# Output projection after attention: split products in the last head, late rows last, and a later rounding of x

## What is computed

```
xn  = layernorm(x)                                  # 2048 x 1024
qkv = xn @ attn_qkvw + attn_qkvb
ctx = softmax(q k^T / sqrt(32)) v   for 32 heads     # columns side by side: 2048 x 1024
z   = xn @ A_w^T                                     # 2048 x 512
gate = softmax of the 16 largest of 64 router scores, 0 elsewhere
out = x + ctx @ attn_ow + attn_ob + 2 * (z * gate) @ B_w^T
```

## Time and profile before

| what | us |
|---|---|
| three runs, median | 2524.45 |
| the profiled execution, its own time | 2530.7 |
| its span, first to last instruction | 2528.9 |
| PE busy | 2489.5 (98%) |
| DVE / ACT / POOL busy | 1493.7 / 1224.9 / 1636.1 |
| end of the last-head matmuls | 2247.8 |
| first matmul of the output stage | 2254.6 |
| mean granted TensorE clock | 0.994 |

### The profile page before, as it was taken

The page is one execution under the profiler, slowest core; times in us unless marked ns, Lnnn a source line. Parts: engine busy times, 40 slices in busy tenths (PEclk is TensorE's granted clock), DMA queues, the critical chain, the costliest instruction groups (busy, mean ns, idle before and its releaser), DMA issues. The chain is left out here.

```text
span 2528.9 us, 34185 instructions
## 1 busy us (share of the span) xinstructions
PE 2489.5 (98%) x12856; PEld 1622.4 (64%) x12856; DVE 1493.7 (59%) x2524; ACT 1224.9 (48%) x2311; POOL 1636.1 (65%) x556
## 2 busy tenths in 40 slices
PE   7999999999999999999999999999999999989999
PEld 4788888888755555555555555555555555448887
DVE  7511110104588788788888788878888888522221
ACT  5211111110066676667666666667666766761000
POOL 0110111221079999999999999999999999962121
PEclk9999999999999999999999999999999999999999
DMA  4233335324367777777877877877777777564332
GB/s 167 92 125 124 124 115 162 102 79 125 96 158 164 150 160 165 158 151 165 165 150 158 165 153 155 167 150 161 164 159 150 166 165 151 116 158 141 116 104 88
DMA packets 174991, 359.26 MB, mean 142 GB/s; under 512 B 90432, under 2 KB 115520, under 8 KB 143808
## 3 DMA queue, kind: packets, MB, share of 16 engines
q0 software_dynamic: 22752, 165.69, 33.2%
q1 hardware_dynamic: 152096, 191.70, 26.5%
HBM read 127.42 MB, written 63.70 MB: 76 GB/s over the span
## 5 line engine op out<-in xcount | busy, mean ns | idle before, releaser
L1173 DVE TENSOR_REDUCE part_max<-ps_b 128x1 f32<-128x512 f32 x1984 | 1214.4, 681 | 263.7 <-PE ps_b L1046 263.6
L997 POOL TENSOR_TENSOR psum_p<-psum_p,probs 128x2048 f32<-128x2048 f32 x253 | 1181.8, 4671 | 53.6 <-ACT probs L1159 43.3
L1159 ACT ACTIVATE probs<-ps_b 128x512 f32<-128x512 f32 x1920 | 971.2, 621 | 351.2 <-PE ps_b L1036 345.9
L1036 PE MATMUL ps_b<-q,k 97*128 97x512 f32 x1344 | 547.6, 412 | 0.0
L1046 PE MATMUL ps_b<-k,q 96*128 96x512 f32 x1344 | 536.8, 401 | 0.6
L1036 PEld LDWEIGHTS ps_b<-q,k 97*128 97x128 f32 x1344 | 252.4, 188 | 223.4 <-issue 135.8
L1064 PE MATMUL ps_b<-probs,v 128*32 128x512 f32 x2640 | 319.4, 598 | 0.5 <-ACT probs L1159 0.5
L351 POOL TENSOR_TENSOR wlo<-wraw,whi 128x1024 fp32r<-128x1024 f32 x20 | 48.0, 2399 | 405.7 <-ACT whi L512 405.7
L1036 PE MATMUL ps_b<-qk 97*128 97x512 f32 x704 | 289.8, 414 | 2.0 <-PEq L84 1.7
L1046 PEld LDWEIGHTS ps_b<-k,q 96*128 96x128 f32 x1344 | 256.4, 191 | 49.5 <-DVE part_max L1173 17.9
L1046 PE MATMUL ps_b<-qk 96*128 96x512 f32 x640 | 254.8, 398 | 0.0
(11 more groups left out here) (128 smaller groups left out, 2572.6 us busy)
## 6 DMA issues: line engine op xcount, KB each, us to landing
psum_q<-probs POOLq DMA_DIRECT2D x158, 1024.0 KB, 7.7
qk<-qk_scr SPq DMA_DIRECT2D x66, 256.0 KB, 7.3
qk_scr<-ehi SPq DMA_DIRECT2D x16, 1024.0 KB, 3.9
qk_scr<-elo SPq DMA_DIRECT2D x16, 1024.0 KB, 6.7
k<-qk_scr SPq DMA_DIRECT2D x63, 256.0 KB, 4.1
q<-qk_scr SPq DMA_DIRECT2D x63, 256.0 KB, 8.0
wraw<-wcat SPq DMA_DIRECT2D x21, 512.5 KB, 7.4
craw<-cz_scr SPq DMA_DIRECT2D x14, 768.0 KB, 4.8
```

Of the source, the lines that this page charges most:

```text
L997: pool.tensor_tensor(acc[:, :], first[:, :], tile(h, t)[:, :], ALU.add).then_inc(pool_done, 1)
L1036: pe.matmul(ps[:, st_bank(n), :], kp[s][0:PACK + 1, t * P:(t + 1) * P], qp[s][0:PACK + 1, b * NQ:(b + 1) * NQ], start=True, stop=True).the ...
L1159: act.activation(tile(h, t)[:, b * NQ:(b + 1) * NQ], ps[:, st_bank(n), :], ACT.Exp, scale=SCALE).then_inc(exp_done, 1)
L1173: dve.tensor_reduce(part_max[hn % 2][:, tn, b:b + 1], ps[:, ring_bank(u), :], AX_X, ALU.max) \
```

## The change

- **x rounded later.** In pass n ACT does `normalise(n-1)`, then `round_x(n-3)`, then `deviation(n)`; DVE does `rest_x(n-4)` where it did `rest_x(n-3)`, and the copies of the router's query come one pass later.
- **First splits in the last head.** In head 31 ACT makes `chi` of row blocks 0 to 5 of token tile 0 after tile 6 (after `take_sums(30)`), and `whi` of weight blocks 0 and 1 after tiles 7 and 8. DVE makes the `clo` and the two `wlo` at tile 9, before the reciprocal of head 30.
- **The sums' way of head 31** moves into the output stage: ACT copies the sums there, SP spreads them behind two weight loads, the reciprocal comes after `wlo` of block 6, and the product with the raw context goes from POOL to DVE, behind `clo` of token tile 1. POOL's `normalise(30)` comes after its additions; its result is stored by SP in the output stage.
- **Late rows last.** PE does row blocks 0 to 10 of both token tiles, then row block 11 of both.
- Tiles are placed elsewhere so that the new writes touch only free memory; seven weight blocks are loaded early instead of six; PSUM is one tensor for both stages, and token tile 1 uses banks away from the sums.

```
             for n in range(TT):
-                if n >= CHUNK:
-                    round_x(n - 2)
                 if n >= 1:
                     normalise(n - 1)
+                if n >= ROUND_LAG:          # ROUND_LAG = 3
+                    round_x(n - ROUND_LAG)
                 deviation(n)
-                if 2 <= n < CHUNK:
-                    round_x(n - 2)
...
                 if n >= 1:
                     shift(n - 1)
-                if n >= 3:
-                    rest_x(n - 3)
+                if n > ROUND_LAG:
+                    rest_x(n - ROUND_LAG - 1)
                 variance(n)
-                if n >= CHUNK and n % CHUNK == CHUNK - 1:
-                    router_query(n // CHUNK - 1)
+                if n > CHUNK and n % CHUNK == 0:
+                    router_query(n // CHUNK - 2)
...
# attend, SP
-            store_ctx(LAST - 1)
-            for s in range(2):
-                sp.wait_ge(ctx_stored[s], 16 * QB * (HEADS // 2 - (LAST % 2 == s)))
-            sp.wait_ge(sums_taken, HEADS)
-            for b in range(QB):
-                sp.dma_start(sums_q[b * HD:(b + 1) * HD, :], sums_b[b * HD:b * HD + 1, :]).then_inc(last_spread, 16)
# attend, POOL
                 for t in LAST_POOL_ORDER if h == LAST else POOL_ORDER:
-                    if h == LAST and t == LAST_POOL_TILES[-1]:
-                        normalise(LAST - 1)
...
+            normalise(LAST - 1)
# attend, ACT (SPLIT_AT = SUMS_AT = 6, SPLIT_W = 2, FIRST_KT = 6, before 4)
                     if t == SUMS_AT and h >= 1:
                         take_sums(h - 1)
+                    if h == LAST and t == SPLIT_AT:
+                        act.wait_ge(ready_loaded[0], 16)
+                        act.wait_ge(pv_done, TT * (LAST - 1))
+                        act.activation(chi[:, 0, 0:FIRST_KT, :], craw[:, 0, 0:FIRST_KT, :], ACT.Copy).then_inc(chi_part, 1)
+                    if h == LAST and t - SPLIT_AT - 1 in range(SPLIT_W):
+                        k = t - SPLIT_AT - 1
+                        act.wait_ge(early_loaded, 16)
+                        act.wait_ge(sum_ready, LAST)
+                        act.activation(whi[:, k, :], w_early[:, k, :], ACT.Copy).then_inc(whi_done, 1)
             take_raw(LAST)
-            take_sums(LAST)
# attend, DVE
+                    if h == LAST and t == RECIPROCAL_AT:
+                        dve.wait_ge(chi_part, 1)
+                        dve.tensor_tensor(clo[:, 0, 0:FIRST_KT, :], craw[:, 0, 0:FIRST_KT, :],
+                                          chi[:, 0, 0:FIRST_KT, :].bitcast(F32), ALU.subtract).then_inc(clo_part, 1)
+                        for k in range(SPLIT_W):
+                            dve.wait_ge(whi_done, k + 1)
+                            dve.tensor_tensor(wlo[:, k, :], w_early[:, k, :], whi[:, k, :].bitcast(F32), ALU.subtract) \
+                                .then_inc(wlo_done, 1)
                     if t == RECIPROCAL_AT and h >= 1:
                         reciprocal(h - 1)
# output stage, SP (EARLY = 7, before 6)
-            for k in range(EARLY, EARLY + 3):
+            for k in range(EARLY, EARLY + 2):
                 load_w(k)
+            sp.wait_ge(last_taken, 1)
+            for b in range(QB):
+                sp.dma_start(sums_q[b * HD:(b + 1) * HD, :], sums_b[b * HD:b * HD + 1, :]).then_inc(last_spread, 16)
+            for k in range(EARLY + 2, OUT_KT):
+                load_w(k)
+            sp.wait_ge(ctx_ready, LAST)
+            for b in range(QB):
+                sp.dma_start(cz_scr[BOTTLENECK + (LAST - 1) * HD:BOTTLENECK + LAST * HD, b * NQ:(b + 1) * NQ],
+                             out_last[b * HD:(b + 1) * HD, :]).then_inc(ctx_stored[(LAST - 1) % 2], 16)
             sp.wait_ge(last_recip, 1)
...
# output stage, POOL
-            pool.wait_ge(last_recip_loaded, 16 * QB)
-            pool.tensor_tensor(sums_b[:, :], raw_last[:, :], recip_b[:, :], ALU.mult).then_inc(last_ready, 1)
-            pool.wait_ge(last_ready, 1)
# output stage, PE
+            def first_tiles(ks):
+                for u in range(2):
+                    for k in ks:
+...
+                        last = products(u, k)          # six matmuls, after the waits for its splits
+                    if k == OUT_KT - 1:
+                        last.then_inc(mm_ready, 1)
-            tile(0, 0, True)
-            tile(0, 1, True)
+            first_tiles(range(READY_KT))               # READY_KT = 11
+            first_tiles(range(READY_KT, OUT_KT))
# output stage, ACT
-            split_piece(0, 0)
-            split_w(0)
-            split_w(1)
-            split_piece(0, 1)
-            for k in range(2, OUT_KT):
+            act.wait_ge(sum_ready, HEADS)
+            act.wait_ge(sums_spread, 16 * QB * LAST)
+            act.activation(sums_b[:, :], ps[:, sum_bank, :], ACT.Copy).then_inc(last_taken, 1)
+            for k in range(SPLIT_W, OUT_KT):
                 split_w(k)
+                if k == FIRST_KT - 2:
+                    split_piece(0, 1)
             split_piece(1, 0)
# output stage, DVE
-            split_piece(0, 0)
-            split_w(0)
-            dve.wait_ge(last_spread, 16 * QB)
-            dve.reciprocal(recip_q[:, :], sums_q[:, :]).then_inc(last_recip, 1)
-            split_w(1)
-            split_piece(0, 1)
-            for k in range(2, OUT_KT):
+            for k in range(SPLIT_W, OUT_KT):
                 split_w(k)
+                if k == FIRST_KT - 2:
+                    split_piece(0, 1)
+                if k == FIRST_KT:
+                    dve.wait_ge(last_spread, 16 * QB)
+                    dve.reciprocal(recip_q[:, :], sums_q[:, :]).then_inc(last_recip, 1)
             split_piece(1, 0)
+            dve.wait_ge(last_recip_loaded, 16 * QB)
+            dve.tensor_tensor(sums_b[:, :], raw_last[:, :], recip_b[:, :], ALU.mult).then_inc(last_ready, 1)
```

More of the change, by code:

```diff
@@ L540, in _ @@
                     round_w(1, 1, 1)
-            round_x(TT - 2)
             normalise(TT - 1)
-            round_x(TT - 1)
+            for n in range(TT - ROUND_LAG, TT):
+                round_x(n)
             def q_part(u, blk, nb):
@@ L725, in attend @@
 def attend(nc, qk_scr, v_scr, recip_scr, cz_scr, w2, w_early, early_loaded, qk0, q12, k12, v01, part_max0,
-           z3_stored, craw, ready_loaded, tail):
+           z3_stored, craw, ready_loaded, tail, w2_split, chi, clo, split_done, seam):
     with ExitStack() as ctx:
@@ L737, in attend @@
         qp = [qk0[:, 0, :], q12[:, 0, :], q12[:, 1, :]]
[L738 to L742, removed]
+        whi, wlo = w2_split
+        psum_p, psum_q, probs = [], [], []
+        for n_tiles in (OUT_KT // 2 - 1, RING - OUT_KT // 2 + 1):
+            (psum_p if not psum_p else psum_q).append(sb(f"psum_{len(probs)}", [P, T]))
+            for _ in range(n_tiles):
+                probs.append(sb(f"probs{len(probs)}", [P, T]))
+        psum_p.append(sb("psum_p1", [P, T]))
+        psum_q.append(sb("psum_q1", [P, T]))
+        raw_last, sums_b, recip_b, sums_q, recip_q, out_last = tail
         raw_ctx = [raw_last if s == LAST % 3 else sb(f"raw_ctx{s}", [P, NQ]) for s in range(3)]
         out_ctx = [sb(f"out_ctx{s}", [P, NQ]) for s in range(2)]
+        vh = [v01[:, 0, :, :], v01[:, 1, :, :], sb("vh2", [P, TT, HD])]
         ones = sb("ones", [P, HD])
@@ L1203, in _, with project_output @@
                         take_transposed(h + 1)
-def project_output(nc, x, w2, bias, cz_scr, w_early, early_loaded, ehi, chi, clo, ob, w_last, v01, recip_scr, craw,
-                   ready_loaded, tail, out):
+    return ring_bank(("sum", LAST, 0, 0))
+def project_output(nc, x, w2, bias, cz_scr, w_early, early_loaded, ehi, chi, clo, ob, w_mid, w_last, recip_scr, craw,
+                   ready_loaded, tail, w2_split, split_done, seam, sum_bank, out):
     with ExitStack() as ctx:
@@ L1319, in _, with products @@
         def _(pe):
-            def tile(i, u, first=False):
-                if not first:
-                    pe.wait_ge(chi_done, 2 * i + u + 1)
-                    pe.wait_ge(clo_done, 2 * i + u + 1)
-                wait(pe, res_ready, 2 * i + u - 1)
-                n = 0
-                for k in range(OUT_KT):
-                    if first:
+            def products(u, k):
+                for n, (c, w) in enumerate(((chi, whi), (chi, wlo), (clo, whi))):
+                    for b in range(2):
+                        last = pe.matmul(ps[:, first_bank[u] + b, :], c[:, u, k, :], w[:, k, b * NQ:(b + 1) * NQ],
+                                         start=(k == 0 and n == 0), stop=(k == OUT_KT - 1 and n == 2))
+                return last
+            def first_tiles(ks):
+                for u in range(2):
+                    for k in ks:
                         for n_piece, (k0, k1) in enumerate(PIECES[u]):
@@ L1331, in tile @@
                                 pe.wait_ge(*piece_done(u, n_piece, clo_part, clo_done))
-                    if first and u == 0:
-                        pe.wait_ge(whi_done, k + 1)
```

(22 more changed lines are left out.)

80 lines of the change are left out of this document (45 added, 35 removed).

## The result

The changed kernel is slower. Six runs gave 2530.68 to 2535.17 us, median 2533.37; six runs of the kernel before beside them 2520.17 to 2528.88, median 2524.82. The ratio is 1.0033 with a 95% interval of [1.0018, 1.0048], some 8 us. Run once more (experiment 10) it was 1.0035 [1.0022, 1.0049]. The forecast was 2521.9, range 2513 to 2529.

The account below looks back on a forecast made before the run. PE was taken as the bound, its idle and low-clock time winnable. Input stage -4.2 plus tile 2's start +1.6 gave -2.6 us: 2528.1 against the profiled execution, 2521.9 as median; range 2513 to 2529.

Parts of the forecast that it names:

- The 3.95 us of idling go: Output stage, before block 11 of tile 0: PE's 3.95 us wait disappears, with 8.5 us to spare.
- the -2.6: Whole kernel: -4.2 from the input stage plus 1.6 from tile 2's later start, taken off the 2524.45 us median.
- What is late next: Output stage: tile 2's load stands uncovered behind tile 0's result; 8.5 us idling, 2.8 low-clock loss, net +1.6 us.
- Splits in head 31: Last head: ACT waits 1.9 us for `craw`, its list grows 4.6 us, PE ends attention 3.5 us later.
- rival C: Last head: the load of `craw` lands 7.4 us later, giving 2530.8 us with the clock's full drop; chance 0.12.
- The clock in head 31: Last head: PE's 2.9 us standstill may drop the clock, costing 0 to 2.1 us; entered as +0.6.
- Start of the output stage: First output block: starts 0.65 us after PE, the last engine; clock stays up and most of 2.8 us loss goes.
- Late rows last: Output stage, block 11 of both first tiles: sums ready at 2275, needed at 2283.5; tile 1 ends 9.7 us sooner.
- x rounded later: Input stage: ACT no longer waits for transposes, PE becomes the bound; -4.2 us, bounds -2.5 to -6.
- rival D: Input stage: PE, DVE or the clock's rise takes the gain back, leaving +1.6, 2526 us; chance 0.16.

Follow-up runs that it names:

- experiment 10: The changed kernel once more, unaltered: 2531.12 us, ratio 1.0035 to the kernel before.
- old rounding: The changed kernel with the input stage's rounding of x as in the kernel before: 2533.26 us, ratio 1.0055 to the kernel before.
- Experiment 6: The kernel before with only PE's order changed, row blocks 0 to 10 of both first tiles, then block 11 of both: 2534.17 us, ratio 1.0047.
- Experiment 4: The changed kernel with the context load moved ahead of the wait for the result's read: 2521.84 us, ratio 1.0002 to the kernel before.
- Experiment 3: The changed kernel with head 31's splits later and DVE's reciprocal ahead of its subtractions: 2525.91 us, ratio 1.0016 to the kernel before.
- experiment 1: The kernel before with only the later rounding of x: 2520.64 us beside 2522.57, ratio 0.9995.

## Why the prediction was wrong

The seam between attention and the output stage, by stretch (us of the profiled spans). "To sums" runs from the first score matmul of attention to the copy of head 30's sums, then comes the stretch to PE's first output matmul, then to tile 2's first, then to the end. Tile 2's start of the kernel before is that of its 145th output matmul.

| kernel, span | attention starts | to sums | to output | to tile 2 | to end |
|---|---|---|---|---|---|
| before, as forecast from, 2528.9 | 695.52 | 1523.7 | 35.4 | 41.3 | 233.0 |
| before again, 2519.1 | 691.96 | 1523.3 | 36.1 | 34.8 | 232.9 |
| forecast | 691.3 | 1523.7 | 33.5 | 42.0 | 235.8 |
| after, 2531.0 | 691.54 | 1523.3 | 37.5 | 44.1 | 234.6 |
| after again, 2526.7 | 690.94 | 1524.1 | 34.4 | 41.7 | 235.5 |
| old rounding, 2530.9 | 695.49 | 1523.6 | 34.2 | 42.0 | 235.6 |
| order only, 2533.9 | 695.45 | 1523.4 | 35.3 | 43.9 | 235.9 |

The second execution of the changed kernel lies within 1 us of the forecast in every stretch, and its span of 2526.7 is 0.4 from the forecast one (2528.9 - 2.6 = 2526.3). That closeness is in part luck: it was the fastest of its five runs, 2.7 us below their median, and some of its stretches are over the forecast, some under. The first execution was 4.7 over it. The measured median is 11.5 us over the forecast median (2533.37 against 2521.9): 6.2 are the step from the profiled execution to the median, 4.7 are in the stretches of the table, and 0.5 is what the profiled execution of the changed kernel lay below its median.

- **The step that failed: "The 3.95 us of idling go", and the -2.6 then taken off the median.** The 3.95 us and the 1.7 of low clock behind it came from one 8.80 us product of POOL that took 1.53, 1.46 and 1.68 in the three other profiles in which POOL makes it. So the execution that was forecast from carried 5.6 us that the others don't, and lay 6.2 above the median. The forecast took them off twice: once as something the change removes, once in going over to the median. Against an execution without them, the stretch to tile 2 grows from 34.8 to 41.7 or 44.1, where the forecast had 41.3 growing to 42.0. Experiment 6 shows it by itself: some 9 us there and 3.0 to the end. That every execution near the median is without them is not shown: it rests on three profiles.
- **What is late next** was right in mechanism and near in size: 8.5 us of idling forecast, 8.43 to 8.75 measured in the four profiles with this order in which DVE's split took 1.76, 10.82 in the one where POOL's addition started first and the split took 3.70. The low clock behind it was forecast at 2.8; the stretch to the end grew by 1.7 to 3.0. Experiment 4 closes it.
- **Splits in head 31.** Mechanism right, size low in the landing of `craw`: 5.5 us taken from one row, where the second execution of the same kernel has 11.2. From issue to chi it was 10.3, 7.7, 6.8, 8.7 and 11.2 us in the five profiles where ACT waited. This is rival C, which "decides from a landing 2.6 us later than before": true in three of five. PE stood still 3.8 to 8.0 us instead of 2.9. C's time, 2530.8, was closest to the truth, but by luck: it was added to the same median, and its mechanism makes the smaller part of the loss: the second execution of the changed kernel was 0.9 over the forecast in this stretch, the first 4.0. Experiment 3 removes the wait.
- **The clock in head 31** did drop (0.50 from 2219 to 2227); +0.6 was entered as a probability. The Trainium skill (TensorE: Matmul & The Clock Gate, Part 1: The HAM clock gate) lists the low level as that of an idle engine. The trace agrees for the pause of 7.16 us, and for the one of 4.58 in the second execution (0.56 granted from 2221 to 2223, when PE had just started again).
- **Start of the output stage**: 0.65 us after PE was forecast, 0.61 measured, clock up. Right.
- **Late rows last**: cover 8.5 us forecast, 7.6 measured (2275.14 to 2282.75). Right, and worth nothing in the second execution of the kernel before, where PE did not wait for them.
- **x rounded later.** Stretches of 15.15, 13.53 and 13.11 us between router blocks, against 15.1, 13.6 and 13.0 forecast:

```profile
26.16:41.31 15.15, 14.54 (x72) 10.11 (x73) 12.28 (x29) 9.31 (x13) 0.00 (x0) 0.88 0.46 139
41.31:54.84 13.53, 12.91 (x72) 9.59 (x73) 12.29 (x29) 9.32 (x14) 0.00 (x0) 1.00 0.36 123
54.84:67.95 13.11, 12.03 (x65) 8.66 (x66) 5.49 (x8) 6.73 (x9) 0.00 (x0) 1.00 0.01 2
```

  The first block, however, starts 2.1 us later (26.16 for 24.04) where 0.6 was said, so 2.6 us arrive at the end of the stage. And of these little is left: attention started at 691.96 in the second profile of the kernel before and at 689.7 to 691.7 in ten with the later rounding. In three profiles with the old rounding it started at 695.5. The granted clock tells them apart. In those three it was at 0.50 for 6.8 us between 81 and 90 us, behind the 32 small matmuls for the keys, although PE was busy without a pause from 78 to 92 us. In the second profile of before it stayed at 1.00, and in the ten it was low for 3.4 us or not at all. The two of these ten without a low stretch start attention at 689.66 and 690.49, 1.5 to 2.3 us before the second profile of the kernel before. So the gain of 4.0 us against the execution of the forecast is in part the clock's, and this term too was smaller against an execution nearer the median. Whether the old rounding brings the longer low stretch about more often is open; experiment 1 (0.9995 [0.9985, 1.0006]) says that the later rounding is not worth 0.2% here. This is rival D, in part.

**Left open.** Why the identical load of `craw`, with the accumulating load of `psum_q` issued beside it, takes from 5.5 to 11.2 us. Why POOL's product stands behind all of DVE's queued subtractions once and gets in between them three times, although DVE had started 0.7 to 0.9 us ahead of it in all four. The runs of the kernel before fall into a group near 2520 and one near 2525, and what parts the groups is not shown. Two things of that size differ between profiles: the low stretch before attention (3.5 us), and the late product for head 30 in experiment 1, whose execution of 2525.07 us has 40.1 us in the stretch to the output where the second profile of the kernel before has 36.1. The placements of the tiles and the seventh early weight block were not tried alone.

## What to carry to other kernels

Before a wait is counted as a gain, look whether the profiled execution lies above the median: what it has too much may be that very wait, and then it must not be taken off the median as well. Here a second profile of the unchanged kernel showed both what the forecast had wrong: no wait of 3.95 us, and a landing of 11.2 us for 5.5. A reordering that gives one transfer cover takes it from another: ask which load is started by the result that now comes later, and separate the parts of that load that need not wait.

## What the runs showed of the hardware

- At the end of a block POOL's drain ended 4.0 us after POOL's last instruction, in all fourteen profiles of this study (3.96 to 4.05), whether that was a 128x512 product or a 128x2048 addition. Where it came last, PE started 0.5 to 0.6 us after it. Where PE itself came last, it started 0.61 to 0.64 us after its own end.
- In the output stage DVE's subtraction of 1536 columns and POOL's addition of 1024 overlap in 126 places of the fourteen profiles. In the 100 where DVE started first (by 0.00 to 1.01 us) it took 1.76 us and POOL 3.01 to 4.01. In the 26 where POOL started first (by 0.03 to 0.31 us) POOL took 2.34 to 2.40 and DVE 3.70 to 3.97. The instruction that started first kept its time, and the other paid, without an exception.
- In a row of queued subtractions the start does not decide: a 128x512 product of POOL beside them took 8.80 us once and 1.46 to 1.68 in three other executions of the same code. The other way round, two subtractions of 1024 columns took 10.64 us beside POOL's additions of 2048 columns, instead of 2.35:

```profile
2225.72 10.64 DVE L1210 TENSOR_TENSOR w2lo<-w_early,w2hi 128x1024 fp32r<-128x1024 f32 x2 [1.94 <-ACT w2hi L1171]
...
2261.36 2.35 DVE L1425 TENSOR_TENSOR w2lo<-w_late,w2hi 128x1024 fp32r<-128x1024 f32 x2
```
